# Two-layer graph network on one core: the x products begin in tile 1, the scales are made in tiles 1 and 2

## The reference

```
# block 1: two layers, each relu([h, neigh(h)] @ W.T + b)
for W, b in ((W0, b0), (W1, b1)):
    h = relu(concat([h, segment_mean(h[dst] over src)], 1) @ W.T + b)
x = layernorm(x + h)
# block 2: h_self + mean over edges of the 32 largest entries of h_neigh
y = x @ W_self + segment_mean(maxk(x @ W_neigh, 32)[src] over dst)
out = layernorm(x + y)
```

## Time and profile before

| | |
|---|---|
| median of three runs | 675.32 us |
| the profiled execution | 673.44 us |
| its span, first to last instruction | 671.6 us |
| TensorE busy | 635.9 us, 95% of the span |
| VectorE (DVE) busy | 498.8 us, 74% |
| ScalarE (ACT) busy | 314.5 us, 47% |
| GpSimd (POOL) busy | 110.0 us, 16% |

### The profile page before, as it was taken

The page is one execution under the profiler, slowest core; times in us unless marked ns, Lnnn a source line. Parts: engine busy times, 40 slices in busy tenths (PEclk is TensorE's granted clock), DMA queues, the critical chain, the costliest instruction groups (busy, mean ns, idle before and its releaser), DMA issues.

```text
span 671.6 us, 10824 instructions
## 1 busy us (share of the span) xinstructions
PE 635.9 (95%) x3782; PEld 323.6 (48%) x3783; DVE 498.8 (74%) x1274; ACT 314.5 (47%) x604; POOL 110.0 (16%) x187
## 2 busy tenths in 40 slices
PE   8788899999978999999999899999999999999996
PEld 3466566666533444444444344444444444444442
DVE  7888979999778888888863678787887846633333
ACT  3678799999667766666641222222222210000000
POOL 3001122222111110101000232323223110000000
PEclk9989999999999999999999999999999999999999
DMA  8543644555612222322223999999999933300000
GB/s 215 101 141 110 218 138 159 166 181 162 186 56 58 60 56 56 60 53 65 50 60 95 165 208 174 206 177 186 192 173 187 178 90 116 116 25 26 27 25 23
DMA packets 66741, 79.61 MB, mean 119 GB/s; under 512 B 30320, under 2 KB 59407, under 8 KB 66681
## 3 DMA queue, kind: packets, MB, share of 16 engines
q1 hardware_dynamic: 66681, 78.86, 54.9%
HBM read 38.91 MB, written 33.38 MB: 108 GB/s over the span
## 4 chain that ended last, share of the span: by engine, by line
PE 66%; DVE 15%; DMA 9%; ACT 4%; issue 3%; POOL 2%; SPq 1%; DVEq 0%; POOLq 0%; ACTq 0%
PE pair L1550 23%; PE bank L1648 10%; PE pair L1648 10%; PE bank L1474 6%; DMA tr_sb<-part 5%; PE bank L1445 4%; PE pair L1365 4%; PE bank L1453 3%; PE pair L1453 3%; DMA own_in<-own_dram 2%; DVE m L953 2%; DVE hots L648 2%; DVE work L958 2%; POOL part L556 1%; DVE tree L831 1%
## 5 line engine op out<-in xcount | busy, mean ns | idle before, releaser
L1550 PE MATMUL pair<-xs,ct 125*128 125x512 f16 x625 | 139.4, 379 | 2.3 <-issue 2.3
L1550 PE MATMUL pair<-a,ct 125*128 125x512 f16 x625 | 138.9, 379 | 0.0
L648 DVE TENSOR_TENSOR hots<-iota,jobs 125x1792 f16<-125x1792 f16 (+1 forms) x100 | 103.6, 1069 | 3.4 <-PE pair L1365 2.9
L1550 PEld LDWEIGHTS pair<-xs,ct 125*128 125x128 f16 x625 | 61.7, 99 | 75.0 <-issue 2.8
L1550 PEld LDWEIGHTS pair<-a,ct 125*128 125x128 f16 x625 | 62.0, 99 | 73.8
L1079 ACT ACTIVATE slab<-pair 125x875 f16<-125x875 f32 (+1 forms) x100 | 83.3, 854 | 11.3 <-PE pair L1365 6.8
L1231 ACT ACTIVATE a<-ct 125x1000 f16<-125x1000 f16 (+1 forms) x75 | 80.4, 1072 | 9.7 <-DMA c_dram<-slab 8.1
L538 POOL TENSOR_TENSOR own_in<-own_in,bias_sb 125x256 f32<-125x256 f32 x50 | 37.8, 757 | 246.5 <-DMA own_in<-own_dram 246.5
L1648 PE MATMUL bank<-xs,ct 125*128 125x512 f16 (+1 forms) x325 | 71.5, 379 | 0.0
L1648 PE MATMUL pair<-xs,ct 125*128 125x512 f16 x300 | 66.2, 379 | 0.0
L1299 ACT ACTIVATE sd<-mv,epsb 125x1 f32<-125x1 f32 x25 | 7.4, 294 | 113.9 <-DVE mv L1015 113.9
(11 more groups left out here) (202 smaller groups left out, 758.4 us busy)
## 6 DMA issues: line engine op xcount, KB each, us to landing
c_dram<-slab SPq DMA_DIRECT2D x25, 683.6 KB
ct<-c_dram SPq DMA_DIRECT2D x25, 683.6 KB
own_in<-own_dram SPq DMA_DIRECT2D x50, 125.0 KB
own_dram<-own SPq DMA_DIRECT2D x25, 125.0 KB
own_dram<-own_st SPq DMA_DIRECT2D x25, 125.0 KB
x_in<-in_x_dram SPq DMA_DIRECT2D x25, 125.0 KB
z_dram<-z_st SPq DMA_DIRECT2D x25, 125.0 KB
a<-z_dram SPq DMA_DIRECT2D x5, 625.0 KB
```

The costliest lines, as they stand in the source:

```text
L648: v.tensor_tensor(hots[k][:, :, :, :].rearrange("p w g (a d) -> p (w g) a d", d=2), iota, job, ALU.is_equal).then_inc(win_hot, 1)
L1550: ins = mm(agg[k % 3][0:lhs.shape[1], :], lhs, parts[l][:, t, :], start=t == 0, stop=t == NT - 1, skip_group_check=True)
```

## The change

Products of x start in tile 1: one each in tiles 1 and 2, two in tile 3, and one in each tile from 4 on. The first product is copied out unscaled, and POOL multiplies it with the scale when that is ready. The scales are made in tiles 1 and 2. All four pieces of x are bounded by squares on ACT, the reductions of weights move ahead of the loop or to its start, and `wneigh`, `wself` and the bias are loaded ahead of the last two pieces of x. The idle matmuls in tiles 1 to 3 go. The stores of the split weights go to tiles 4 and 5, and ACT's wait for them to just ahead of the last copy of tile 8.

```
-TWOS = (8, 12, 16, 20)
-OWN = {t: [] for t in range(4)}
-for _t in range(4, NT):
-    _n = sum(map(len, OWN.values()))
-    OWN[_t] = [_n, _n + 1] if _t in TWOS else [_n]
+OWN = {1: [0], 2: [1], 3: [2, 3]}
+OWN.update((_t, [_t]) for _t in range(4, NT))
 PACK = 128
-KEEP = {0: 4, 1: 2, 2: 2, 3: 2}
+KEEP = 4
...
-            for c in range(4):
+            def load_x_piece(c):
...
+            load_x_piece(0)
+            load_x_piece(1)
             sp.dma_start(wn_nat[:, :, :], wneigh.rearrange("(h p) k -> p h k", p=128)).then_inc(wn_loaded, 16)
             sp.dma_start(ws_nat[:, :, :], wself.rearrange("(h p) k -> p h k", p=128)).then_inc(ws_loaded, 16)
             sp.dma_start(bcol[:, :], b0.rearrange("(h p) -> p h", p=128),
                          allow_slow_non_contiguous=True).then_inc(b_loaded, 16)
+            load_x_piece(2)
+            load_x_piece(3)
...
             def store_own(t):
-                sp.wait_ge(own_copied, t + 2)
+                if t:
+                    sp.wait_ge(own_copied, t + 2)
+                else:
+                    sp.wait_ge(own_scaled, 1)
                 sp.dma_start(own_dram[t], own[:, t % 2, 0:F]).then_inc(own_stored[t % 2], 16)
             for t in range(NT - 1):
-                for o in OWN[t]:
-                    store_own(o)
+                if t == 2:
+                    store_own(0)
+                if t == 3:
+                    store_own(1)
+                    store_own(2)
+                if t == 4:
+                    store_own(3)
+                if t > 3:
+                    store_own(t)
                 store_slab(t)
-                if t == HELD - 2:
-                    sp.wait_ge(w_split, 4)
-                    for l in range(2):
-                        sp.dma_start(wparts_dram[l], w_parts[l][:, :, :, :].rearrange("p h q f -> p (h q f)")
-                                     ).then_inc(w_stored, 16)
-            for o in OWN[NT - 1]:
-                store_own(o)
+                if 3 < t < 6:
+                    sp.wait_ge(w_split, 2 * t - 6)
+                    sp.dma_start(wparts_dram[t - 4], w_parts[t - 4][:, :, :, :].rearrange("p h q f -> p (h q f)")
+                                 ).then_inc(w_stored, 16)
+            store_own(NT - 1)
...
                 pool.wait_ge(own_copied, t + 2)
+                if t == 0:
+                    pool.wait_ge(scale_ready, 1)
+                    nc.gpsimd.tensor_tensor(own[:, 0, :], own[:, 0, :], scales[0:P, 1:2].broadcast_to([P, 2 * F]), ALU.mult
+                                            ).then_inc(own_scaled, 1)
+                    pool.wait_ge(own_scaled, 1)
                 a0 = own[:, t % 2, F:2 * F]
...
-            for l in range(2):
-                for h in range(2):
-                    at = 6 + 2 * l + h
-                    v.tensor_reduce(stat[:, at:at + 1], w_nat[:, l, h, :], X, ALU.add, apply_absolute_value=True).then_inc(w_sums, 1)
+            def sum_w(l, h):
+                at = 6 + 2 * l + h
+                v.tensor_reduce(stat[:, at:at + 1], w_nat[:, l, h, :], X, ALU.add, apply_absolute_value=True).then_inc(w_sums, 1)
+
+            def largest_wn():
+                dve.wait_ge(wn_loaded, 16)
+                v.tensor_reduce(stat[:, 12:14], wn_nat[:, :, :], X, ALU.max, apply_absolute_value=True
+                                ).then_inc(stat_ready, 1)
+
+            def largest_ws():
+                dve.wait_ge(b_loaded, 16)
+                v.tensor_reduce(stat[:, 14:16], bcol[:, :].rearrange("p (h o) -> p h o", o=1), X, ALU.max,
+                                apply_absolute_value=True).then_inc(stat_ready, 1)
+                dve.wait_ge(eye_added, 2)
+                v.tensor_reduce(stat[:, 10:12], ws_nat[:, :, :], X, ALU.max, apply_absolute_value=True
+                                ).then_inc(stat_ready, 1)
+
+            sum_w(0, 0)
+            sum_w(0, 1)
+            sum_w(1, 0)
             unpack(0)
...
             quick_hots(0, 3)
+            sum_w(1, 1)
+            largest_wn()
             unpack(1)
...
             quick_hots(1, 3)
+            largest_ws()
...
                     if more:
                         quick_hots(t + 1, 0)
                     if t == 1:
-                        largest_x(3)
+                        bound_rows()
                     if t == 2:
                         dve.wait_ge(cols_copied, 4)
-                        bound_rows()
                     tr_copy(t - 1, 1)
+                    if more:
+                        quick_hots(t + 1, 1)
+                    if t == 2:
+                        scales_out()
                     if 3 < t < 6:
                         w_low(2 * t - 8)
                     if more:
-                        quick_hots(t + 1, 1)
+                        quick_hots(t + 1, 2)
                     if t == 1:
-                        largest_w()
-                    if t == 3:
-                        scales_out()
-                    if 3 < t < 6:
-                        w_low(2 * t - 7)
-                    if more:
-                        quick_hots(t + 1, 2)
-                    if t == 2:
                         bounds()
                     if more:
                         quick_hots(t + 1, 3)
                     tr_copy(t - 1, 3)
+                    if 3 < t < 6:
+                        w_low(2 * t - 7)
...
+            act.sem_inc(own_copied, 1)
+            for i in range(2):
+                act.sem_inc(own_stored[i], 16)
...
             slots_out(0)
+            act.wait_ge(const_ready, 10)
+            square_x(0)
             jobs_out(0)
-            act.wait_ge(const_ready, 11)
-            square_x(0)
+            square_x(1)
             slots_out(1)
             quick_copy(0, 0)
             quick_copy(0, 1)
-            square_x(1)
+            square_x(2)
             quick_copy(0, 2)
...
+            def own_first():
+
+                act.wait_ge(own_done, 1)
+                a.activation(own[:, 0, :], bank[6][0:P, :], ACT.Copy).then_inc(own_copied, 1)
+
             def own_copy(t, par, m):
 
                 act.wait_ge(own_done, t + 1)
+                act.wait_ge(scale_ready, 1)
...
-            def ready_for_own():
-                act.wait_ge(unscale_ready, 4)
-                act.sem_inc(own_copied, 1)
-                for i in range(2):
-                    act.sem_inc(own_stored[i], 16)
...
             def quick_copies():
                 quick_copy(0, FILLS - 1)
-                square_x(2)
+                square_x(3)
                 for t in range(1, NT):
-                    if t == HELD:
-                        act.wait_ge(w_stored, 32)
                     own = OWN[t]
                     quick_copy(t, 0)
-                    if t == 4:
-                        ready_for_own()
+                    if t == 1:
+                        own_t(0)
                     tr_copy(t - 1, 0)
                     quick_copy(t, 1)
-                    if own:
+                    if t > 2:
                         own_copy(own[0], own[0] % 2, own[0] // 2)
-                    if own and own[0] + 1 < NT:
-                        own_t(own[0] + 1)
+                        if t + 1 < NT:
+                            own_t(own[0] + 1)
                     if 3 < t < 6:
                         w_high(2 * t - 8)
                     quick_copy(t, 2)
                     tr_copy(t - 1, 2)
                     if 3 < t < 6:
                         w_high(2 * t - 7)
+                    if t == HELD:
+                        act.wait_ge(w_stored, 32)
                     quick_copy(t, 3)
-                    if t == 3:
-                        own_t(0)
-                    if len(own) > 1:
-                        own_copy(own[1], own[1] % 2, own[1] // 2)
-                        if own[1] + 1 < NT:
-                            own_t(own[1] + 1)
+                    if t == 1:
+                        own_first()
+                    elif t < 4:
+                        own_copy(own[-1], own[-1] % 2, own[-1] // 2)
+                    if t < 4:
+                        own_t(own[-1] + 1)
                 for g in (0, 2):
...
             def bounds_t():
-                pe.wait_ge(squared, 3)
-                pe.wait_ge(stat_ready, 4)
+                pe.wait_ge(squared, 4)
+                pe.wait_ge(stat_ready, 3)
                 pe.wait_ge(w_sums, 4)
...
+            def next_transposes(t):
+
+                if t in XC:
+                    pe.wait_ge(x_loaded[XC.index(t)], BOTH)
+                own_transposes(t, xs32[:, t, :])
+
...
                     fill(t, 0)
-                    if t == 2:
+                    if t == 1:
+                        next_transposes(0)
                         bounds_t()
-                    if t in KEEP:
-                        keep_clock(bank[7], KEEP[t])
-                    if own:
+                    if t > 2:
                         own_product(own[0], 0)
                     transposes(t - 1, par, 0)
```

(51 more changed lines are left out.)

35 lines of the change are left out of this document (2 added, 33 removed).

## The result

The changed kernel takes 665.49 us (median of four executions; 663.18 to 668.73) against 675.37 us for the kernel before, run beside it (674.93 to 677.57): ratio 0.985, 95% interval 0.982 to 0.988. The forecast was 668.0 us with a range from 664.5 to 672.0, and "faster", meaning under 671.9 us, at 0.85. The profiled execution took 663.18 us in all, 10.26 less than that of before.

The account below looks back on a forecast made before the run. DVE was taken to set the pace in tiles with one product, TensorE close behind. -10.3 + 2.5 + 0.2 + 0.3 = -7.3 us, from the median of 675.32 to 668.0 us; range 664.5 to 672.0.

Parts of the forecast that it names:

- From tile 4 on, -10.3: Second products of tiles 8, 12, 16, 20 and the wait for stored weights go: 10.3 us gained if single tiles keep 5.18.
- rival 3: Single tiles don't keep 5.18 us over a long row; 0.2 us more in each of 18 gives 671.6 us; chance 0.08.
- The early products, +2.5: Tiles 1 to 5: products there spend TensorE's lead, DVE waits in tiles 3 and 4, tile 6 starts 2.5 us later.
- Rival 4: TensorE gets to tile 3 early enough, its lead isn't lost and the 2.5 us go: 665.5 us; chance 0.10.
- those put ahead of `w_low`: Tiles 4 and 5: DVE waits of 0.6 us for the inputs of `w_low`.
- The prologue, +0.2: Before the loop: the moved square and reductions fill waits, so lateness is paid; 0.2 us taken, up to 1.5.
- The two filled places: Before the loop: ACT's 1.75 us wait ahead of `jobs` takes a square, DVE's 1.30 us wait takes two reductions.
- POOL's scaling, +0.3: At about 47 us: 1.5 us of POOL beside DVE's one-hot sets costs 0 to 0.6 us, 0.3 taken.
- Behind the stage, 0: What follows the changed stage keeps its length and moves as a whole.
- Rival 1, the clock: TensorE's clock stays at 1.2 GHz until product 0 has run in tile 1: +1.9, so 669.9 us; chance 0.26.
- Rival 2, low to the end of tile 3: TensorE's clock stays low through tile 3: +12.5 - 7.3, so 680.5 us, slower; chance 0.06.
- Rival 5: Prologue late by up to 1.5 us, or new waits of tiles 2 to 5 cost 2 us more: 670 us; chance 0.10.

Follow-up runs that it names:

- run 8: Changed kernel with products 3 to 11 one tile later, so the pair of products stands in tile 12 and not tile 3; one execution, 667.48 us.
- run 3: Changed kernel with the stores of the split weights and ACT's wait for them back in their old places; 668.03 us, ratio 0.987 to the kernel before.
- run 7: Changed kernel with every product from 3 on one tile later, the pair in tile 24; 664.11 us, ratio 0.985 to the kernel before.
- run 2: Kernel before without its idle matmuls in tiles 1 to 3; 674.91 us, ratio 1.000.
- run 4: Kernel before with only the new order of loads: `wneigh`, `wself` and bias ahead of pieces 2 and 3 of x; one execution, 677.27 us.
- run 11: Changed kernel with idle matmuls ahead of tile 1 and around the first picks, pair in last tile, POOL's scaling behind all four scales; 662.30 us, ratio 0.981.
- run 1: Kernel before with only the new places of the split weights' stores and of ACT's wait for them; 672.35 us, ratio 0.996.
- run 10: Changed kernel with six idle matmuls ahead of tile 1, and more ahead of the first pick and behind its first four; 664.57 us, ratio 0.983.
- run 5: Changed kernel measured again, nothing edited; 666.64 us, ratio 0.987 to the kernel before.
- run 9: Changed kernel with 24 idle transposes on TensorE in its pause ahead of tile 1; 663.66 us, ratio 0.982 to the kernel before.
- run 6: Changed kernel with six idle matmuls on TensorE where it stands still ahead of tile 1; 664.83 us, ratio 0.984 to the kernel before.

## Why the prediction was right, and which terms were off

The forecast's mechanism held and its sum was 2.9 us too small against the profiled execution (7.3 forecast, 10.2 found): 1.5 in the early products with POOL's scaling, 0.5 in the prologue, 0.9 behind the stage. By its steps:

- **From tile 4 on, -10.3.** Found -10.29; single tiles keep 5.15 to 5.2 us over 18 tiles, so rival 3 is out. Of the parts, the stores alone gave 2.63 (2.6 forecast), and run 8 gives back the 7.09 us of a tile with a pair. Put back into the changed kernel the stores cost 1.4 (run 3), so the parts don't simply add.
- **The early products, +2.5.** This term was mis-sized. From the start of tile 1 to that of tile 6 the trace loses 1.26. Its mechanism is shown: TensorE is busy all the time in tiles 3 and 4, and run 7 removes just the second wait. The pair alone costs 1.82 (run 7); that the whole loses less fits the 0.9 us that the idle matmuls had cost in tiles 1 to 3 (run 2). Rival 4, that no lead is lost, falls with that; that its number (665.5) is the one measured is chance. What the plan had wrong is how late TensorE gets there. Tile 1 came out 0.34 us shorter than laid out by hand, tile 3 0.61 (its first wait is 1.12 and not 1.9, its last 0.4 isn't there), tiles 4 and 5 together 0.51 (the wait of tile 4 is 1.24 and not 1.85, and those put ahead of `w_low` don't come); tile 2 was 0.25 longer. The copy of the scales came at 46.05 us and not at 46.7, as the squares were done by 34.5 and not 34.8; by DVE's first copy of tile 3 the plan was 0.8 late (52.36 instead of 53.2).
- **The prologue, +0.2.** Found -0.27. The two filled places cost nothing: the square of piece 0 is done at 18.35 us, and DVE waits 0.75 us for `jobs` instead of 0.55, but with one reduction less ahead of it starts its sets 0.2 earlier; ahead of `held_row` it waits 0.32 instead of 1.30 and starts at the same time (24.79). What the plan passed over is a gain: of the loads it said only that they would be in time, and the earlier one of `wself` takes POOL's additions out of DVE's way (the operations named at run 4).
- **POOL's scaling, +0.3.** Found nothing by the first set of tile 4. It took 1.04 us and not 1.5. What it held up is a product of scales of two elements, 0.90 us instead of 0.16: it ends at 47.42, POOL's operation at 47.40. The Trainium skill (SBUF — State Buffer, section SBUF: two separate sides) says that a DVE operation with two inputs in SBUF and a GpSimd operation that reads SBUF lock a shared pair of ports against each other for a whole instruction; these two ends agree. In run 11, where the small product is free of it, tile 2 is 0.1 us shorter than in run 7 and tile 3 as much longer: in tile 3 DVE waits 1.1 us for TensorE anyway. No run has the kernel without the scaling.
- **Behind the stage, 0.** Found -0.90; what was to move as a whole didn't, and the plan has no term for it. The pause at the start of layer 1 (TensorE, "issue") is 2.33 us in the profile of before and 1.23 after, but layer 1 as a whole is only 0.23 shorter, and runs 1 and 2, the kernel before with one edit, have the short pause (1.19 and 1.27) and not the shorter time (502.6 and 502.5 from the set of tile 23 to the end, where before took 502.68). The larger part, 0.64, lies in layer 2, where TensorE waits for the loads of `tr_sb`: from its first matmul to the first of the last sum it takes 174.0 to 174.1 us in the four profiles with the old products and 173.0 to 173.7 in eight of the nine with the new (175.7 in run 3). That speaks for this part going with the change; what in the change does it isn't shown.
- **Rival 1, the clock.** It isn't the result's profile, but it is real: of nine profiles with products in tile 1, three (runs 3, 8, 10) show the clock at 0.50 up to 44 us or later, with product 0 at 3.7 to 3.8 us (3.6 laid out) and tile 1 at 11.05, 11.14 and 11.52 us against 9.73. Its price was put at 1.9; tile 1 alone gives 1.3 to 1.8, tiles 1 and 2 together 1.6 to 2.1. Whether it comes is settled by the execution and not by the kernel alone: run 3 has it, and the result and run 5, with the same instructions up to there, have not. The Trainium skill (TensorE: Matmul & The Clock Gate, section Part 1: The HAM clock gate) calls the warm-up variable from run to run; these three profiles agree. The rule that transposes don't count as activity the way matmuls do was not settled (runs 9 to 11).
- **Rival 2, low to the end of tile 3.** In none of the nine; the latest return is at 46 to 47 us. Falls at 52 to 56 us stand in three profiles of the kernel before with an edit (runs 1, 2, 4), where tiles 3 and 4 still have pauses; in the nine, with TensorE busy without a gap from 50 to 60 us in the result's, in none. That the pauses are the cause isn't shown.
- **Rival 5** is out: no new wait of tiles 2 to 5 beyond the two foreseen.

What stays open: why layer 2 is shorter, what in an execution decides at which pause the clock falls, and whether the change makes it fall more or less often. The median is 9.9 us better and the profiled pair 10.3, so a large difference in what the two kernels pay for it is unlikely.

## What to carry to other kernels

Where one engine sets the pace and a second stands close behind it, spread the second's work evenly: a product that is doubled in one tile cost 1.8 to 1.9 us here, also in tile 3, which looks as if it had a lead. The cheap place for it was the last tile, where DVE has no sets left to make: 0.8 us. If an edit changes the end of a stage, read its gain at the end of that stage: behind it, profiles of these kernels differ by as much again. Lay such a stage out by hand with the lengths from the trace, but expect the waits of the plan to add up too high (here 0.3 us too late at the squares, 0.65 at the scales, 0.8 in tile 3). And look at the granted clock of several executions before a profile is taken for the kernel: two profiles of one kernel lay 3 us apart, by a fall of the clock ahead of the loop.

## What the runs showed of the hardware that was not expected

TensorE's granted clock is either 1.00 or 0.50 here (2.4 or 1.2 GHz), and at the same pause of the same kernel it falls in some executions and not in others: at 15 us in the profile of run 5 and not in that of the result, and in seven of eleven profiles without the edit of run 10. It fell there in neither of the two with it, which is few. A fall costs about 3 us there, since DVE and ACT wait for the picks. In tiles 1 and 2 a short one costs 0.8 us against run 6, which has none (16.08 and 15.25 us), and a long one about 2.5 to 2.9 (runs 3, 8 and 10). Tile 4 took 1.35 us more with one (run 1), tile 8 2.75 (run 2). An operation of two elements on DVE took 0.90 us instead of 0.16 where POOL had started first.
